# Another order in the feed-forward's second half and in the first tile of attention

## The reference

```python
x = x + attn(layernorm(x), w_qkv, b_qkv, w_o, b_o)        # softmax(q k / 4) v, 16 heads
...
def act_quant(x):                       # one scale for each row
    scale = 127.0 / clip(max(abs(x)), 1e-05)
    return clip(round(x * scale), -128, 127) / scale
def bitlinear158(x, w, b):              # x / rms(x), quantized; ternary weights
    return einsum('bsd,od->bso', act_quant(rms_norm(x)), weight_quant(w)) + b
h = silu(bitlinear158(layernorm(x), w1, b1))    # 256 -> 1024
h = layer_norm(gelu(h), ln_g, ln_b)
x = x + bitlinear158(h, w2, b2)                 # 1024 -> 256
```

## Time and profile before

| | us |
|---|---|
| median of 3 runs (835.77 to 838.88) | 835.78 |
| the profiled execution | 838.17 |
| its span, first to last instruction | 835.5 |

### The profile page before, as it was taken

One profiled execution on the slowest core, in us unless ns is written; L12 is line 12 of the kernel. 1 busy time (PEld: TensorE's weight loads), 2 busy tenths in 40 slices (PEclk: granted clock), 3 DMA queues, 4 the chain that ended last, 5 costly groups with the idle time before them and its releaser, 6 DMA issues. The chain is left out here.

```text
span 835.5 us, 15110 instructions
## 1 busy us (share of the span) xinstructions
PE 677.7 (81%) x4160; PEld 450.1 (54%) x4163; DVE 566.5 (68%) x1180; ACT 396.9 (48%) x895; POOL 338.3 (40%) x658
## 2 busy tenths in 40 slices
PE   4999999979999799789995868888897589255555
PEld 3677777744444455467774556665664334043333
DVE  2888888856999663233224898787886566378775
ACT  1566666640000572053320646555555276777773
POOL 0223222335775233411114443223223566488884
PEclk9999999999999698799997999999999599656755
DMA  8804000002321501252211020000000000000101
GB/s 306 352 2 149 25 0 0 1 1 38 50 50 38 201 1 38 77 182 67 82 53 57 26 102 2 2 0 0 0 1 1 2 0 0 0 1 0 50 0 50
DMA packets 23016, 41.90 MB, mean 50 GB/s; under 512 B 3041, under 2 KB 18033, under 8 KB 21825
## 3 DMA queue, kind: packets, MB, share of 16 engines
q1 hardware_dynamic: 19488, 31.14, 11.9%
q0 software_dynamic: 3488, 10.28, 3.4%
HBM read 31.15 MB, written 10.26 MB: 50 GB/s over the span
## 5 line engine op out<-in xcount | busy, mean ns | idle before, releaser
L216 POOL TENSOR_TENSOR var_eps<-mv,powers 128x1 f32<-128x1 f32 x96 | 19.5, 203 | 251.2 <-DVE mv L211 251.1
L300 PE MATMUL ps<-ident,work 128*128 128x128 f32 x512 | 78.7, 276 | 19.6 <-ACT wide L432 19.6
L656 PE MATMUL ps<-ctxT,small 128*128 128x512 f32 x192 | 84.9, 602 | 1.2 <-ACT xnT_all L629 0.8
L432 ACT COPY wide<-ps 128x512 f32<-128x512 f32 x128 | 75.1, 587 | 21.9 <-PE ps L300 21.8
L499 DVE TENSOR_REDUCE work<-ps 128x8 f32<-128x1024 f32 x64 | 78.0, 1218 | 10.9 <-PE ps L293 10.4
L502 DVE TENSOR_TENSOR work<-ps,work 128x1024 f32<-128x1024 f32 x64 | 78.4, 1225 | 6.0 <-DVE work L499 1.2
L293 PE MATMUL ps<-wide,work 64*128 64x512 f32 x256 | 73.2, 648 | 9.4 <-DVE work L502 6.9
L300 PEld LDWEIGHTS ps<-ident,work 128*128 128x128 f32 x512 | 58.7, 141 | 35.3 <-issue 18.4
L427 ACT ACTIVATE work<-work 128x1024 f32<-128x1024 f32 x64 | 67.9, 1061 | 13.6 <-DVE work L502 13.0
L695 POOL TENSOR_TENSOR ctxT<-xn_all 128x1024 f32 (+1 forms) x32 | 59.9, 1893 | 25.3 <-PE ps L656 25.3
L656 PEld LDWEIGHTS ps<-ctxT,small 128*128 128x128 f32 x192 | 36.5, 193 | 47.8 <-issue 45.6
(11 more groups left out here) (195 smaller groups left out, 1589.5 us busy)
## 6 DMA issues: line engine op xcount, KB each, us to landing
wide<-in_expert_gu SPq DMA_DIRECT2D x1, 4096.0 KB, 21.1
small<-hank SPq DMA_DIRECT2D x32, 128.0 KB, 3.8
sorted_x<-small POOLq DMA_DIRECT2D x1, 2944.0 KB, 10.4
work<-sorted_x SPq DMA_DIRECT2D x23, 128.0 KB, 2.0
sorted_y<-work POOLq DMA_DIRECT2D x23, 128.0 KB, 2.1
xn_all<-in_ctx_rev_t SPq DMA_DIRECT2D x1, 2048.0 KB, 11.1
wide<-in_expert_d SPq DMA_DIRECT2D x1, 2048.0 KB, 26.8
ctx_sb<-in_ctx SPq DMA_DIRECT2D x1, 2048.0 KB, 8.1
```

The costliest lines, as they stand in the source:

```text
L300: mm = pe.transpose(T[:, h * P:(h + 1) * P], prob[r][:, h * P:(h + 1) * P], ident)
L432: act.copy(probT[r], T).then_inc(s["pT"], 1)
L656: mm = pe.matmul(ps[4 * u + o], toep[u][:, c, lt * P:(lt + 1) * P], kv[u][:, c, half * 512:(half + 1) * 512], start=(c == 1 - lt), stop=(c ...
```

## The change

Three things. The loads of constants get a semaphore each, and those of qk_cols and of_head are issued behind the attention weights; each engine waits only for what it reads. Before attention's loop TensorE makes queries, keys, the transpose of tile 1 and then values; ScalarE copies both transposed tiles before the values, and VectorE sets the ones behind both normalizations. In the feed-forward, the bias is added to x by GpSimd in the first half, at the end of its step; in the second half VectorE's step becomes centring t, update of x t-3, ln t, largest t-1, inverse t-1, largest magnitude t, rounding t-1, and GpSimd's becomes reciprocal deviation t+1, mean t+2, factors and unscale t-1, rms t, without inv_unscale. The counts of the semaphore factor follow (`made`), and ScalarE's squares of t wait for the epsilon of t-1 instead of t-2.

```diff
@@ attention @@
             def tensor(pe):
-                pe.wait_ge(const_loaded, 16 * N_CONST)
+                pe.wait_ge(ident_loaded, 16)
                 before(pe)
                 front_transpose(pe, f, 0, 0, X)
                 pe.wait_ge(attn_loaded[layer], 16)
                 pe_q(pe, 0, 0)
-                pe_v(pe, 0, 0)
                 pe_k(pe, 0, 0)
                 front_transpose(pe, f, 1, 1, X)
+                pe_v(pe, 0, 0)
...
             def scalar(act):
-                act.wait_ge(const_loaded, 16 * N_CONST)
                 before(act)
+                front_copy(act, f, 0, 0, X, s["v_ps"], B)
+                act.wait_ge(cols_loaded, 32)
+                act_q(act, 0, 0)
+                front_copy(act, f, 1, 1, X, s["v_ps"], B)
                 act.wait_ge(s["ones"], 2 * layer + 2)
-                front_copy(act, f, 0, 0, X, s["v_ps"], B)
-                act_q(act, 0, 0)
                 act_v(act, 0, 0)
-                front_copy(act, f, 1, 1, X, s["v_ps"], B)
...
             def vector(dve):
-                dve.wait_ge(const_loaded, 16 * N_CONST)
                 before(dve)
-                for u in range(2):
-                    dve.memset(va[u], 1.0).then_inc(s["ones"], 1)
                 for t in range(2):
                     front_stats(dve, f, t, t)
                     front_xn(dve, f, t, t)
                     beside("dve", dve, t - 2)
+                for u in range(2):
+                    dve.memset(va[u], 1.0).then_inc(s["ones"], 1)
+                dve.wait_ge(cols_loaded, 32)
                 dve_keys(dve, 0, 0)
...
@@ feed_forward @@
+            def made(k, t):
+
+                return 3 * t if k == 0 else 3 * NB + 2 * t
...
                 pool.tensor_tensor(factor[u], inverse[u], rms127[u], ALU.mult).then_inc(s["factor"], 1)
-                wait(pool, s["diag"], n - 1 if k == 0 else NB)
-                pool.tensor_tensor(inv_unscale[u], inverse[u], inv_wk[:, k:k + 1], ALU.mult
-                                   ).then_inc(s["factor"], 1)
+                if k == 0:
+                    wait(pool, s["diag"], t - 1)
+                    pool.tensor_tensor(inv_unscale[u], inverse[u], inv_wk[:, k:k + 1], ALU.mult
+                                       ).then_inc(s["factor"], 1)
...
                 if there(t):
                     pool_unscale(pool, t, u, 0, (s["silu"], 2 * (t - 1)))
+                    pool.wait_ge(f.xn, f.base + t + 1)
+                    pool.tensor_tensor(tile_of(x, t), tile_of(x, t), row_bias[:, 2 * D:3 * D],
+                                       ALU.add).then_inc(s["x_bias"], 1)
...
                     act.wait_ge(s["ln"], t + 1)
-                    wait(act, s["eps"], NB + t - 1)
+                    wait(act, s["eps"], NB + t)
...
@@ dve_second @@
                                              ).then_inc(s["centred"], 1)
-                if there(t - 1):
-                    dve_largest(dve, t - 1, 1 - u, 1)
                 if there(t - 3):
...
                                              ).then_inc(s["x_new"], 1)
-                if there(t - 1):
-                    dve_inverse(dve, t - 1, 1 - u, 1)
                 if there(t):
...
                                              ).then_inc(s["ln"], 1)
                 if there(t - 1):
-                    dve.wait_ge(s["factor"], 3 * (NB + t - 1) + 1)
-                    wait(dve, s["qT_ps"], NB + t - 2)
-                    dve.tensor_scalar(q32[1 - u], Ht(t - 1), factor[1 - u], MAGIC, ALU.mult,
-                                      ALU.add).then_inc(s["rounded"], 1)
+                    dve_largest(dve, t - 1, 1 - u, 1)
+                if there(t - 1):
+                    dve_inverse(dve, t - 1, 1 - u, 1)
                 if there(t):
...
                                       ).then_inc(s["abs"], 1)
+                if there(t - 1):
+                    dve.wait_ge(s["factor"], made(1, t - 1) + 1)
+                    wait(dve, s["qT_ps"], NB + t - 2)
+                    dve.tensor_scalar(q32[1 - u], Ht(t - 1), factor[1 - u], MAGIC, ALU.mult,
+                                      ALU.add).then_inc(s["rounded"], 1)
...
             def pool_second(pool, t, u, i):
-                if there(t - 1):
-                    pool_factors(pool, t - 1, 1 - u, 1)
-                    pool_unscale(pool, t - 1, 1 - u, 1, (s["x_new"], t - 3))
                 if there(t + 1):
                     pool_rstd(pool, t + 1, 1 - u)
                 if there(t + 2):
                     pool_mean(pool, t + 2, u)
-                if there(t):
-                    pool.tensor_tensor(tile_of(x, t), tile_of(x, t), row_bias[:, 2 * D:3 * D],
-                                       ALU.add).then_inc(s["x_bias"], 1)
+                if there(t - 1):
+                    pool_factors(pool, t - 1, 1 - u, 1)
+                    pool_unscale(pool, t - 1, 1 - u, 1, (s["x_new"], t - 3))
+                if there(t):
                     pool_rms(pool, t, u, 1)
...
@@ sync_loads @@
-            for dst, src in ((powers, a["powers"]), (ident, a["ident"]),
-                             (of_head, a["of_head"]), (qk_cols, a["bias_cols"])):
-                sp.dma_start(dst, src).then_inc(const_loaded, 16)
+            sp.dma_start(powers, a["powers"]).then_inc(powers_loaded, 16)
+            sp.dma_start(ident, a["ident"]).then_inc(ident_loaded, 16)
             sp.dma_start(w_qkv3[0], cp(a["w_qkv0"])).then_inc(attn_loaded[0], 16)
+            for dst, src in ((qk_cols, a["bias_cols"]), (of_head, a["of_head"])):
+                sp.dma_start(dst, src).then_inc(cols_loaded, 16)
```

More of the change, by code:

```diff
@@ L161, in build @@
         attn_loaded = [sem("attn0_loaded"), sem("attn1_loaded")]
-        const_loaded = sem("const_loaded")
+        powers_loaded, ident_loaded, cols_loaded = sem("powers_loaded"), sem("ident_loaded"), sem("cols_loaded")
         moe_y = sem("moe_y")
@@ L591, in gpsimd @@
             def gpsimd(pool):
-                pool.wait_ge(const_loaded, 16 * N_CONST)
+                pool.wait_ge(powers_loaded, 16)
                 front_rstd(pool, f, 0, 0)
@@ L1402, in pool_rms @@
                 pool.wait_ge(s["rms"], n + 1)
-                wait(pool, s["factor"], 3 * (n - 1))
+                wait(pool, s["factor"], made(k, t - 1))
                 pool.tensor_tensor(rms127[u], rms[u], c_127, ALU.mult).then_inc(s["rms127"], 1)
@@ L1410, in dve_largest @@
                 dve.wait_ge(s["abs"], n + 1)
-                wait(dve, s["factor"], 3 * (n - 1))
+                wait(dve, s["factor"], made(k, t - 1))
                 dve.tensor_scalar(largest[u], absmax[u], rms[u], 1e-5, ALU.mult, ALU.max
@@ L1593, in dve_second @@
                     dve.wait_ge(s["x_bias"], t - 2)
-                    dve.wait_ge(s["factor"], 3 * (NB + t - 2))
+                    dve.wait_ge(s["factor"], made(1, t - 2))
                     dve.scalar_tensor_tensor(tile_of(x, t - 3), Y[1 - u][:, 0:D], unscale[1 - u],
```

1 line of the change is left out of this document (removed).

## The result

| | before | after |
|---|---|---|
| median of the device time | 836.0 us | 808.0 us |
| profiled execution | 838.17 | 808.03 |
| its span | 835.5 | 805.6 |
| first scores of the first layer start | 17.45 | 12.75 |
| first L656 | 186.1 | 180.8 |

The ratio is 0.9666, 95% interval 0.9633 to 0.9699. On two further occasions it was 0.9655 and 0.9662. The forecast of 819 was 11 us too long, and 808 lies outside its range of 812 to 828.

What follows compares the result with a forecast made beforehand. The second half was taken as bound by a VectorE-GpSimd ring, no engine full. Terms -2.8 - 2.0 + 4.0 - 16.8 = -17.6 gave 820.6 from the profiled execution, 818.2 from the median; forecast 819 us, range 812 to 828.

Steps and rivals of the forecast that it cites:

- start of the first layer: First attention layer: earlier statistics and keys before values bring first scores from 17.45 to 14.0; 2.8 us of that kept.
- start of the second layer: Second attention layer: ones off the path, 1.03 us, and values behind the keys; -2.0 us (1.0 to 2.3).
- first half: Feed-forward's first half: GpSimd's added bias add delays the factor, 0.27 us for each of 15 tiles, +4.0.
- second half: Feed-forward's second half: 5.4 us a tile instead of 6.48, first to last tile 80.1 instead of 97.2, 17.1 us less.
- drain: Work behind the last tile: ends in the same three-step ring (transposes, conversions, product; 4.95 us a turn), 0.3 us longer.
- the surcharge for the lock: First half: the add runs into VectorE's normalization, which holds off the factor up to 0.2 us further.
- The rival that ends slower: First half: a blocked add takes 1.72 us instead of 0.73, +19; with the ring not opened 845 us; chance 0.04.
- the main step: Second half: the new order opens the ring through GpSimd, so VectorE's own list is the next bound, lower end 5.1 us.
- The ring: Second half of the kernel before: inverse, GpSimd's whole list, largest, inverse wait on each other, setting 6.48 us a tile.
- lock as bound: Rival, second half: GpSimd gets in only when VectorE holds nothing, 5.9 us a tile, 825 us in total; chance 0.18.
- ring not opened: Rival, second half: some wait of the new order ties the engines again, 6.2 us a tile, 829 us; chance 0.08.
- The better side: Rival: 5.1 us a second-half tile, first-half add hidden, starts at their upper ends, 810 us; chance 0.08.

Runs made afterwards that it cites:

- e4: The kernel before, unaltered, profiled a second time; 838.3 us.
- e2: The kernel before with only the feed-forward part of the change, loads and attention as before; 817.08 us, ratio 0.9765.
- e5: The kernel before with one edit: GpSimd's add of the output bias moved from the second half to the first; 829.4 us, ratio 0.9852.
- e9: The changed kernel, unaltered, run once more; 811.22 us, ratio 0.9655 to the kernel before.
- e15: The changed kernel, unaltered, on the same chip as the kernels with combined edits; 809.41 us, ratio 0.9662 to the kernel before.
- e8: The changed kernel plus unused 128x128 products, 13 ahead of the first queries and 12 at the second attention layer; 808.07 us, ratio 0.9617 to the kernel before.
- e7: The changed kernel with the old order of the first tile's products (queries, values, keys) in both attention layers; 819.15 us, ratio 0.9734 to the kernel before.
- e10: The changed kernel with GpSimd computing the factor first in each iteration of the second half; 810.37 us, ratio 0.9641 to the kernel before.
- e3: The changed kernel with GpSimd's bias add put back in the second half; 815.91 us, ratio 0.9741 to the kernel before.
- e13: The changed kernel with unused TensorE products at both attention starts, second-half factor first, and bias adds of tiles 4 to 15 behind the first half; 804.95 us, ratio 0.9618.

## Why the prediction was wrong, point by point

| term | predicted | measured |
|---|---|---|
| start of the first layer | -2.8 (2.0 to 3.4) | -4.9 |
| start of the second layer | -2.0 (1.0 to 2.3) | -3.2 |
| first half | +4.0 | +2.2 |
| second half | -17.1 | -20.0 |
| drain | +0.3 | -2.5 |
| sum | -17.6 | -28.4 |

No single term makes the 10.8 us between the sums: the terms were off by 2.1, 1.2, 1.8, 2.9 and 2.8, all towards too long a time.

The first row is the first L656: 186.1, 185.8, 185.5 and 186.6 with the old start (before, e4, e2, e5), 180.8, 181.1 and 181.3 with the new one (after, e9, e15). The second is L1149 first to last: 51.4, 51.1 and 51.0 (e4, e2, e5) against 47.7 and 47.6 (after, e15), all of them with the long scores; without these it is 48.4 against 45.4 (before, e9), so 3.0 to 3.5. The others are from the pair of profiles. -28.4 agrees with the ratio (3.3% of 836 is 28).

**The start** was right in its steps: x awaited alone, statistics at 3.59 instead of the 3.9 worked out, queries at 7.29 as forecast at 7.3. Two sizes failed. After the keys I counted 0.6 and 2.1 us for transpose and values and put the first scores at 14.0; the values started at 11.30 instead of 11.9 and took 1.41, and the scores came at 12.75. By their durations TensorE got to its higher level during the values; before, it stood at the lower one for all three products and the scores. And of the gain I kept 2.8 on the ground that the next scores would wait for queries and keys of tile 1 at 2.05 and 1.92; these took 1.16 and 1.06. e8 shows what filling TensorE's idle time does by itself (1.8 us at the first scores, 1.2 to 3.1 at the first L656), e7 the order (3.1 and 3.3).

**The second layer** gained past its upper end of 2.3, and its two parts were mis-sized in opposite ways. I counted 1.03 us for the ones. Without them statistics start 0.87 us earlier, but the normalization behind them only 0.2: it waits 1.66 us for GpSimd's deviation instead of 1.03, since GpSimd is busy with a gather (L1082) until 2.0 us behind the first L1149, in before as in after. The order of the products, for which I left about 1 us, gave 1.9 to 2.7 (e7).

**The first half** cost +2.2 instead of +4.0. The factor stands 0.88 and 0.86 us behind unscale, where the forecast had 0.85 plus up to 0.2 for the lock:

```profile
684.15 0.19 POOL L1439 TENSOR_TENSOR ffn_cols<-ffn_cols,small 128x1 f32<-128x1 f32 x1 [0.21 <-ACT wide L1463]
684.35 0.72 POOL L1530 TENSOR_TENSOR x<-x,row_bias 128x256 f32 x1
685.03 0.25 POOL L1430 TENSOR_TENSOR ffn_cols<-ffn_cols 128x1 f32<-128x1 f32 x1
```

The add takes 722 to 726 ns in all 16 tiles: it is never held off, and the surcharge for the lock was wrong. Without it my working had 0.17 and 0.22 us more between unscale and factor, and 0.20 and 0.24 came; of that only 0.15 a tile reaches the time, and what covers the rest wasn't followed. The rival that ends slower needed 1.0 us a tile; 2.2 / 15 is 0.15.

**The second half**: the main step held. The ring was opened, and VectorE's own list is the bound (e10). In the form of the forecast, 4.5 + 14 tiles, 77.2 is 5.19 a tile instead of 5.4, close to its lower end of 5.1. That end agrees in part by luck: 5.34 with seven overlaps of 0.07 makes 4.85, not 5.1, and the list itself takes 4.94 (e10); after adds waits of 0.19 us for the factors, which I had ruled out. What failed is the 0.3 us a tile that I charged for the mutual exclusion. I drew it from the earlier trace rows, where an instruction of VectorE was doubled behind one of GpSimd, and took every collision to cost VectorE the rest. Here GpSimd is already blocked when centring or ln ends; its power runs beside the update of x (756.36, 0.48 us as ever), whose large operand comes from PSUM, and its multiplication beside the next short one. The lock thus cost only GpSimd, which had time. It costs VectorE where GpSimd's instruction starts just as VectorE's next large one begins, behind a reduction that shuts nobody out, and e3 is that case: 0.48 a tile. In these rows what stands at the boundary sets which engine pays, and I had not looked at it for each boundary.

The Trainium skill, page "SBUF — State Buffer", section "Who interferes with whom", says that issue order decides who blocks, and that a VectorE instruction with at most one SBUF input outside the two-port modes doesn't contend. The update of x agrees with the second: it takes 0.48 us beside the power. The first can't be read off the recorded starts this closely: in e3 rounding is held where it starts 0.14 us behind the add, and also where it starts 0.05 ahead of it.

The rival "lock as bound", 5.9 a tile, is refuted; "ring not opened", 6.2, did not come either; where the ring does stay closed, in e5, it is 5.81. The better side had 5.1 a tile and 810 in total; I gave it 0.08, and left most of it out of the range. Its 810 is close to 808 in part by luck: it had the add hidden in the first half and no gain in the drain.

**The drain**: I carried over 4.95 us for each turn of its last ring. That is the price at TensorE's lower level, which the row doesn't say by itself; the transposes and product beside it do, at 1.92 and 1.89. In after TensorE still stands at the lower level when the last centring runs (clock 0.50 from 789 to 793 us), rises early in the drain (0.91 from 793.05 to 796.87), and the last turn takes 3.28. Why it rises there isn't shown, and a shorter tile isn't enough: the drain takes 11.9, 11.9 and 12.7 in three profiles of after, but 14.3 to 14.9 in e3, e10 and e13, whose tiles are shorter than before too.

The Trainium skill, page "TensorE: Matmul & The Clock Gate", section "Part 1: The HAM clock gate", says of a kernel's start that one and the same kernel passes to the higher level after a different number of matmuls from run to run. Here that is seen late in the kernel as well: in the drains of after, e9 and e15 (11.9, 11.9 and 12.7 us), and in the long scores that e9 lacks.

The misses at the start and in the drain have one root: durations of TensorE were carried from the kernel before as if they belonged to the instruction. They belong to the instruction and to the level at which it was read.

## What to carry to other kernels

Where two engines shut each other out, go through the boundaries one by one: ask which instruction is already waiting, and who needs its result. A blocked instruction whose result is due late is free; one that starts just where the busy engine's next large one begins may not be. What is moved off a path (the ones) gives only what the next wait leaves: ask what that is. A matmul's duration out of a trace goes into a sum only with the level of the clock at which it ran, and a step that closes gaps on TensorE may halve those behind it. Before work is taken off the fullest engine, look at what would wait next: here half a reduction, 8 us, gave 0.6.

## What was not expected of the hardware

- Blocked GpSimd instructions end shortly after VectorE lets go: in after a multiplication of 0.19 us, blocked, lasts 1.06 and ends 0.05 behind ln (758.07 against 758.02); the power of 0.55 ends 0.41 behind centring (756.85 against 756.44). Neither lengthened VectorE's next instruction.
- 13 unused products of 128x128 in the first 6.4 us took queries from 2.08 to 1.16 and keys from 1.92 to 1.06 us.
- After a pause of 3.59 us TensorE's next scores took 1.69 to 2.08 us in thirteen profiles and 1.13 in four: before and e4 are the same code and differ in it, and so do after and e9.
